# One core, four residual blocks: values and scores of stage one in plain float32, and its engine orders written anew

## The reference

```
ln    = LN(LN(x)); xn = LN(ctx)                       # 256 and 120 rows a batch
q     = ln @ w_q  * 64**-0.5                          # 8 heads of 64
k, v  = split(concat(xn, ln) @ w_kv)                  # 376 rows
attn  = softmax(q @ k.T + mask)                       # 256 x 376 per head
x1    = x + tanh(g_xattn) * LN((attn @ v) @ w_out)
probs = softmax(LN(x1) @ Wr + br); top 2 of 8, capacity 40 per batch and expert
```

## Time and profile before

| | |
|---|---|
| median of 3 runs | 2526.57 us |
| profiled execution | 2525.54 us, span 2523.7 us |
| mean granted TensorE clock | 0.983 |
| stage one | from 0 to about 1350 us |
| stage two | about 1360 to 1850 us |
| busy over the span | PE 94%, PEld 84%, DVE 75%, ACT 54%, POOL 40% |

### The profile page before, as it was taken

One profiled execution on the slowest core, in us unless ns is written; L12 is line 12 of the kernel. 1 busy time (PEld: TensorE's weight loads), 2 busy tenths in 40 slices (PEclk: granted clock), 3 DMA queues, 4 the chain that ended last, 5 costly groups with the idle time before them and its releaser, 6 DMA issues. The chain is left out here.

```text
span 2523.7 us, 56735 instructions
## 1 busy us (share of the span) xinstructions
PE 2370.8 (94%) x17024; PEld 2118.4 (84%) x17024; DVE 1895.3 (75%) x5597; ACT 1367.1 (54%) x3505; POOL 1011.5 (40%) x1418
## 2 busy tenths in 40 slices
PE   4999999999999999999995999999969999999998
PEld 3888888888888888888875999999958888888887
DVE  4787878878787887878774555555539999999997
ACT  4667666666766666676652333334324444544454
POOL 1445555554554555555451000000045555555551
PEclk8999999999999999999997999999989999999999
DMA  7001101010110101010004222222121122111110
GB/s 266 16 19 33 32 19 33 18 34 17 34 31 19 32 19 33 17 35 32 12 18 144 84 76 76 77 89 63 39 81 53 56 63 60 60 58 56 56 53 21
DMA packets 111712, 128.42 MB, mean 51 GB/s; under 512 B 15058, under 2 KB 98505, under 8 KB 111424
## 3 DMA queue, kind: packets, MB, share of 16 engines
q1 hardware_dynamic: 99264, 105.42, 13.1%
q0 software_dynamic: 12288, 21.21, 2.9%
HBM read 84.42 MB, written 54.53 MB: 55 GB/s over the span
## 5 line engine op out<-in xcount | busy, mean ns | idle before, releaser
L388 POOL TENSOR_TENSOR a_prob<-a_prob,a_rden 128x752 f32<-128x752 f32 x256 | 369.8, 1445 | 520.3 <-DVE a_rden L658 488.2
L503 ACT ACTIVATE a_prob<-a_score,a_nmax 128x376 f32<-128x376 f32 x512 | 289.3, 570 | 316.6 <-DVE a_nmax L653 268.2
L1006 PE MATMUL a_values<-a_prob,a_vo 128*128 128x256 f32 (+1 forms) x2304 | 310.7, 289 | 1.3 <-issue 0.8
L1006 PEld LDWEIGHTS a_values<-a_prob,a_vo 128*128 128x128 f32 (+1 forms) x2304 | 284.2, 191 | 9.6 <-issue 1.0
L1281 ACT ACTIVATE e_hidden<-e_first,e_b 128x256 f32<-128x256 f32 x320 | 134.0, 471 | 288.9 <-PE e_first L80 286.0
L664 DVE TENSOR_TENSOR a_prob<-a_turned,a_prob 128x384 fp32r<-128x384 f32 x512 | 258.5, 546 | 27.7 <-ACT a_prob L513 26.1
L653 DVE TENSOR_REDUCE a_nmax<-a_score 128x1 f32<-128x376 f32 x512 | 254.8, 539 | 30.5 <-PE a_score L973 30.5
L80 PE MATMUL e_first<-e_rowsT,e_w 128*128 128x256 f32 x1920 | 240.4, 286 | 1.8 <-issue 1.8
L982 PE MATMUL a_turned<-a_ident,a_prob 128*128 128x128 f32 (+1 forms) x1536 | 213.5, 275 | 28.3 <-POOL a_prob L388 26.7
L80 PE MATMUL e_second<-e_w,e_hidden 128*128 128x256 f32 x1920 | 239.6, 285 | 0.0
L80 PEld LDWEIGHTS e_first<-e_rowsT,e_w 128*128 128x128 f32 x1920 | 236.7, 195 | 2.0 <-issue 2.0
(11 more groups left out here) (207 smaller groups left out, 4989.4 us busy)
## 6 DMA issues: line engine op xcount, KB each, us to landing
slots<-a_y SPq DMA_DIRECT2D x8, 1280.0 KB, 14.0
e_rows<-slots SPq DMA_DIRECT2D x40, 256.0 KB, 3.9
answers<-e_y SPq DMA_DIRECT2D x40, 256.0 KB, 2.3
a_xn<-x SPq DMA_DIRECT2D x32, 256.0 KB, 3.1
w_in<-W SPq DMA_DIRECT2D x16, 512.0 KB, 3.8
a_xr<-x SPq DMA_DIRECT2D x32, 256.0 KB, 2.8
x<-a_x SPq DMA_DIRECT2D x32, 256.0 KB, 2.2
e_w_in<-W SPq DMA_DIRECT2D x16, 512.0 KB, 4.5
```

The costliest lines, as they stand in the source:

```text
L388: nc.gpsimd.tensor_tensor(prob[:, u % 2], prob[:, u % 2], rden[:, u % 2].unsqueeze(2).to_broadcast([P, 2, NKV]), ALU.mult) \
L503: nc.scalar.activation(prob[:, u % 2, a], score[SCORE_AT[u][a]][:, 0:NKV], ACT.Exp, bias=nmax[:, u % 2, a:a + 1], accum_out=den[:, u % 2, ...
L1006: last = nc.tensor.matmul(out, vo[0:rows, p, v, j, m].rearrange("p c d -> p (c d)")[:, a * DH:a * DH + P], prob2[0:rows, m % 2, w, a, j], ...
```

## The change

- `qT`, `kT` and `vo` are plain float32 with one plane; ACT alone copies the projections out of PSUM (`k_high`, `q_high`, `v_out`), and DVE's `lower` is gone. The projections themselves, `output` and `kvin` stay split in three passes.
- `scores` issues one float32 matmul per head instead of three passes. `times_v` issues one float32 matmul per head and row tile; head a writes 64 partitions from 64 a on, so the block of zeros in `vo` is gone. The heads alternate from one matmul to the next.
- Turned probabilities are copied once to `probT` (float32): head 0 by ACT, head 1 by DVE, instead of a high plane by ACT and a low plane by DVE for both.
- `prob`, `nmax`, `den` and `rden` have four buffers instead of two, and the semaphores of scores, maxima, exps and transposes are kept per head.
- The router's logits and counts go to the bank `values`.
- The orders of all engines are written anew: step s holds projections of batch s - 1, the attention of s - 2 (units 0 and 1 begin in the step before), output of s - 3 and routing of s - 4. On the SP queue a step issues the residual load of s - 1, the store of s - 4 and the loads of s + 2. The prologue before the loop is gone, and its one-time work stands in steps 1 and 3; POOL's wait for the zeroed slots stands in step 2.

```diff
-        qT = sb("a_qT", [P, 2, 2, KI, S], F32R)
-        kT = sb("a_kT", [P, 2, 2, KI, NKV], F32R)
-        vo = sb("a_vo", [P, 2, 2, 3, KI, 3, DH], F32R)
-        nmax = sb("a_nmax", [P, 2, 2])
-        den = sb("a_den", [P, 2, 2])
-        rden = sb("a_rden", [P, 2, 2])
-        prob = sb("a_prob", [P, 2, 2, NKV])
-        prob2 = sb("a_prob2", [P, 2, 2, 2, 3, S], F32R)
+        qT = sb("a_qT", [P, 2, KI, S])
+        kT = sb("a_kT", [P, 2, KI, NKV])
+        vo = sb("a_vo", [P, 2, 3, KI, 2, DH])
+        nmax = sb("a_nmax", [P, 4, 2])
+        den = sb("a_den", [P, 4, 2])
+        rden = sb("a_rden", [P, 4, 2])
+        prob = sb("a_prob", [P, 4, 2, NKV])
+        probT = sb("a_probT", [P, 2, 2, 3, S])
...
+            def exps(b, u, a):
+
+                eng.wait_ge(nmax_ok[a], NG * b + u + 1)
+                at_least(eng, turned_ok[a], NG * b + u - 3)
+                nc.scalar.activation(prob[:, u % 4, a], score[SCORE_AT[u][a]][:, 0:NKV], ACT.Exp,
+                                     bias=nmax[:, u % 4, a:a + 1],
+                                     accum_out=den[:, u % 4, a:a + 1]).then_inc(exp_ok[a], 1)
+
+            def turned_out(b, u, a):
+
+                eng.wait_ge(turned_ok[a], NG * b + u + 1)
+                at_least(eng, pv_made, KI * b + u // 2 - 1)
+                nc.scalar.activation(probT[:, u // 2 % 2, a, :, u % 2 * P:(u % 2 + 1) * P], turned_at(a), ACT.Copy) \
+                    .then_inc(prob_ok[a], 1)
+
...
-            def lower(b, p, u):
-
-                eng.wait_ge(proj_high, NU * b + u + 1)
-                src, dst, scale = projection(p, u, 1)
-                high = projection(p, u, 0)[1].bitcast(F32)
-                if scale == 1.0:
-                    low = nc.vector.tensor_tensor(dst, src, high, ALU.subtract)
-                else:
-                    low = nc.vector.scalar_tensor_tensor(dst, src, scale, high, ALU.mult, ALU.subtract)
-                low.then_inc(proj_low, 1)
...
-            def turned_low(b, u):
-                m, i = u // 2, u % 2
...
-                    eng.wait_ge(prob_high, 2 * (NG * b + u) + a + 1)
-                    nc.vector.tensor_tensor(prob_at(m, i, 1, a), turned_at(a), prob_at(m, i, 0, a).bitcast(F32),
-                                            ALU.subtract).then_inc(prob_low, 1)
...
+            def project_k(b, p, m):
...
+                else:
+                    eng.wait_ge(k_hi, KI * b + m)
+                cols = slice(m * P, (m + 1) * P)
+                split_product(nc, work[0][:, 0:NKV], lambda a, k: wkv[:, a, k, cols],
+                              lambda a, k: kvin2[:, p, a, k, :], KD).then_inc(k_made, 1)
...
-                at_least(eng, exp_ok, 2 * (NG * b + u - 1) + 1)
...
-                for w, (plane_q, plane_k) in enumerate(PASSES):
-                    for a in range(2):
-                        rows = slice(64 * a, 64 * a + 64)
-                        nc.tensor.matmul(score[SCORE_AT[u][a]][:, 0:NKV], qT[rows, p, plane_q, m, i * P:(i + 1) * P],
-                                         kT[rows, p, plane_k, m], start=w == 0, stop=False)
-                for a, done in ((0, score_a), (1, score_b)):
+                    eng.wait_ge(k_hi, KI * b + m + 1)
+                    eng.wait_ge(q_hi, 2 * (b + 1))
+                at_least(eng, exp_ok[0], NG * b + u)
+                at_least(eng, exp_ok[1], NG * b + u - 1)
+                for a in range(2):
+                    rows = slice(64 * a, 64 * a + 64)
+                    nc.tensor.matmul(score[SCORE_AT[u][a]][:, 0:NKV], qT[rows, p, m, i * P:(i + 1) * P],
+                                     kT[rows, p, m], start=True, stop=False)
+                for a in range(2):
                     rows = slice(64 * a, 64 * a + 64)
                     nc.tensor.matmul(score[SCORE_AT[u][a]][:, 0:C], firstrow[rows], mask_row[rows, p],
-                                     start=False, stop=True).then_inc(done, 1)
-
-            def turn_prob(b, u):
+                                     start=False, stop=True).then_inc(score_ok[a], 1)
...
-                out = values[:, 0:S]
-                todo = [(a, v, w, j) for a in range(2) for j in range(3) for v, w in PASSES]
-                for n, (a, v, w, j) in enumerate(todo):
-                    rows = P if j < 2 else C
-                    last = nc.tensor.matmul(
-                        out, vo[0:rows, p, v, j, m].rearrange("p c d -> p (c d)")[:, a * DH:a * DH + P],
-                        prob2[0:rows, m % 2, w, a, j], start=n == 0, stop=n == len(todo) - 1)
-                last.then_inc(ctxv_ok, 1)
+                for j, lo, hi in VALUE_ROWS:
+                    for a in range(2):
+                        last = nc.tensor.matmul(values[64 * a:64 * a + 64, 0:S], vo[0:hi - lo, p, j, m, a],
+                                                probT[0:hi - lo, m % 2, a, j], start=j == 0, stop=j == 2)
+                last.then_inc(pv_made, 1)
...
+            def step(s, p):
...
+                if live(s - 2):
+                    turn_prob(s - 2, 3, 0)
+                    turn_prob(s - 2, 3, 1)
+                    scores(s - 2, p, 6)
+                    times_v(s - 2, p, 0)
+                if live(s - 1):
+                    project_q(s - 1, q, 0)
+                if live(s - 2):
+                    scores(s - 2, p, 7)
+                    turn_prob(s - 2, 4, 1)
+                    times_v(s - 2, p, 1)
+                if live(s - 1):
+                    project_k(s - 1, q, 1)
+                    scores(s - 1, q, 0)
+                if live(s - 2):
+                    turn_prob(s - 2, 4, 0)
+                    turn_prob(s - 2, 5, 1)
...
```

More of the change, by code:

```diff
@@ L344, in store @@
                     .then_inc(x1_out[p], 16)
-            batches(eng, step)
-            store(B - 1, 1)
+            def step(s, p):
+                if live(s - 1):
+                    load_residual(s - 1, 1 - p)
+                if live(s - 4):
+                    store(s - 4, p)
+                if live(s + 2):
+                    load(s + 2, p)
+            all_steps(eng, step)
             for p in range(2):
@@ L1045, in router_count @@
                 eng.wait_ge(soft, N_SOFT * (b + 1))
-                eng.wait_ge(exp_ok, 2 * (NG * (b + 2) + COUNTS_U) - 1 if known(b, 0, B - 2) else 2 * NG * B)
+                if not (isinstance(b, int) and b == B - 1):
+                    eng.wait_ge(att_lo, KI * (b + 2))
                 for i in range(QT):
                     for k in range(i + 1):
-                        last = nc.tensor.matmul(count_at[:, i * E0:(i + 1) * E0], tri[:, 0 if k == i else 1],
+                        last = nc.tensor.matmul(values[:, i * E0:(i + 1) * E0], tri[:, 0 if k == i else 1],
```

784 lines of the change are left out of this document (389 added, 395 removed).

## The result

The changed kernel took 2409.03 us (median of 4, 2406.82 to 2413.45) against 2526.11 (2525.29 to 2528.12): ratio 0.9538, 95% interval [0.9521, 0.9554]. The forecast was 2531, its range 2430 to 2620. The profiled run took 2407.79 us, its span is 2405.8.

The account below looks back on a forecast made before the run. PE was taken to bound stage one: 40.2 + 3.5 (scores) - 2.5 (values) + 1.2 (edges) - 2.4 + 0.4 (waits) = 40.4 us a batch, +5 us in all, so 2531 us, range 2430 to 2620.

Parts of the forecast that it names:

- Score slots: Stage one's scores on PE: a unit's four records take 3 slots, 0.95 us; +3.5 us a batch (bounds +0.9 and +6.0).
- Values slots: Stage one's values products on PE: twelve records take 7 slots, 1.61 us against 2.24 with the late start; -2.5 us a batch.
- the rival of full overlap: Scores and values on PE: halves overlap fully, scores 2 slots, values 6; period 37.3 us, 2440 us; chance 0.20.
- three conditions named as proving me wrong: Stage one on PE: score unit not three slots, twelve values records not seven, or PE waits over 1.5 us per batch.
- Column edges: Values products on PE: their new shape makes 22 edges instead of 16, +1.2 us a batch (0 to 1.6).
- Record length: Full-precision product on PE, read from stage three: two records, each 0.216 us at 256 columns, 0.317 at 376.
- Waits: PE in stage one: of 2.4 us waiting a batch, 0.4 stays (bounds 0 and 1.5).
- The sum: PE's period in stage one: work 42.4 us a batch, less 2.4 of waits, plus 0.4 left, gives 40.4 against 40.2.
- The range: Whole kernel: 2430 to 2620 us, to hold 8 in 10; includes full overlap, stalls, serial scores, not serial values.
- Other engines: Stage one: DVE falls from 32.4 to about 22.4 us a batch, ACT from 26.8 to 22.8.
- PE as the bound: Stage one's steady stretch: PE is busy 1149.7 of 1198.0 us, while DVE and POOL wait much longer for others.
- start and end: Stage one's start and the last batch's closing chain: each priced at +-4 us.

Follow-up runs that it names:

- The grouped products: The changed kernel with its six values products issued head 0 (three), then head 1 (three), instead of by turns: 2472.78 us, ratio 0.9769.
- four batches a turn: The changed kernel with four batches in one turn of stage one's loop instead of two, same work and order: 2454.37 us, ratio 0.9686.
- second and third run of the changed kernel: The changed kernel run again unaltered on two other chips, against the kernel before: 2433.91 us (0.9608) and 2430.8 us (0.9612).
- first run: The changed kernel as first measured and profiled, against the kernel before: 2409.03 us, ratio 0.9538.

## Why the prediction was wrong

- **Score slots: the step that failed.** "I take 3 slots, 0.95, on the assumption that records start in the order issued". It is 2: the second half's first record starts 6 ns after the first half's. The next pair starts 0.420 us after the first, and the mask 0.316 after that, so a pair costs 0.316, with 0.10 more at the change of shape. The unit's start to its mask is 0.74 us where 1.05 was forecast. Scores cost 0.9 us a batch more than before, not 3.5. The grouped products refute the assumption itself: starts leave program order by up to three records.
- **Values slots.** "7 slots" is 6 of 0.216: 0.9 us a batch. These two are the rival of full overlap, to which I gave 0.20. Two of the three conditions named as proving me wrong came true; the third, waits over 1.5 us a batch, did not. The Trainium skill, TensorE: Matmul & The Clock Gate, The mechanism, has packed matmuls some 4 ns apart, and the trace agrees with 6 to 7 ns. Its sentence that matmuls never start out of order, on which I leaned, does not hold here for the two halves; the measurement decides.
- **Column edges.** Forecast +1.2 us a batch; the values products themselves show 0.02 us each, 0.1 a batch (1.45 less 6 x 0.216 = 0.15, against 2.24 less 18 x 0.117 = 0.13). They were paying a change of shape already, since they stood behind scores. The forecast had 0.40 us a product beyond its slots (0.10 left over and a quarter of 1.2), so it was 1.0 us a batch too high here. What the prediction cites from the Trainium skill, TensorEngine Tiling (Array Packing), Key Properties, gives no size for the trace to agree with; the sizes are the trace's alone. Two products a batch now stand behind three transposes, and these take 0.47 us (507.29 to 507.76) where they take 0.31 ahead of the full-height output (528.67 to 528.98): 0.3 us a batch of edges that the table has among the transposes.
- **Record length** was read rightly from stage three: 0.216 for 256 columns, 0.316 for 376.
- **Waits.** Forecast: 2.4 us, of which 2.0 go. The size of 2.4 was right, and all of it went. Then 0.87 came anew at the loop's jump, a place I had not looked at, and the transposes in threes cost 0.74, for which the sum had no term. That the net of the four lines is the 2.0 of the forecast is luck. The cause was wrong too: I put it on order, buffers and DVE together. For the scores it is the six subtractions of DVE, 41 us; order and buffers gave nothing.
- **The sum.** 40.4 forecast less 2.6 for scores and 0.9 and 1.0 for values, plus the 0.9 of new idle time, is 36.8; measured 36.75. Over some 32 batches the 3.44 us are 110 of the 118 us of span.
- **The range** ended at 2430 because the case of full overlap was given at 2440 with waits and edges in it. With the edges at their measured price it would have read 37.3 - 1.0 = 36.3 us, 3.9 x 30 less than before, 2409. That this is the measured time is luck, since the period is 36.75.
- **Other engines.** DVE was forecast near 22 us a batch and ACT near 23; they took 26.3 and 24.1 (778.36 and 713.65 of 1088 us). In the old orders with one DMA moved DVE took 23.3 (702.89 of 1068.00). Most of the 3.0 us between the two are DVE's steps beside POOL's normalising.
- **Right:** PE as the bound, the price of a plain float32 product, start and end within 4 us.

What is left open: why the same kernel shows PE's signals late in some executions and not in others; why four batches a turn lost time; how the 23 us that the edits gain only together divide; what limits how far a half may run ahead.

## What to carry to other kernels

Where a product runs on half of the array beside its twin, count slots by the longer half, not by the order of issue, as long as the twin is no more than three records behind, the most that these runs show; and measure it by a grouped and an alternating version of one loop. A split into high and low parts costs more than its passes: an engine has to subtract, and others wait for it. In the scores the subtractions were worth 41 us, while the plain products alone, with the subtractions kept, lost 11 against three passes. Try a precision edit in the old order first: here the reordering that came with it cost 8 to 28 us, and moving one DMA in the old order gained 16.

## What the runs showed of the hardware

- A full-precision product of 64 rows or of 64 columns and its twin overlap entirely: 0.316 us per pair of records at 376 columns, 0.216 at 256.
- A half's record started ahead of three earlier ones of the other half, and none ahead of four.
- At a loop's jump back DVE issued nothing for 2.7 us (before) and 3.2 to 4.1 us (after), ACT for 0.2 and 2.4 to 3.0, PE and POOL under 0.3 in both. Packets of 8 KB on the queue "instruction" fall there.
- While POOL issued four scattering DMAs, about 5 us, PE's signals came up to about 2.3 us late in the second and third run of the changed kernel, and none over 1 us late in the first run and in another execution of the third run's program; wherever else such signals appeared, they stood beside these DMAs too.
- A DVE step between SBUF tiles took 0.47 us alone and 1.50 on average beside POOL's product of 752 columns (`a_x`), another 0.18 and 1.09 (`a_at_b`). Steps that read PSUM took the same beside it (row maximum 0.54).
- After PE had stood 3.1 us (512.33 to 515.46), the clock was granted at 0.57 from 516 to 520 us, near the 1.2 GHz level, and at 1.00 from 520 to 524.
